# Attention 2: gathers issued back to back, and two norm chains placed one tile later on VectorE

## The reference

```
x = x + tanh(g_ffn[0]) * L0_ffn(layernorm(x))        # rows routed to 8 experts
x = x + tanh(g_xattn[1]) * L1_xattn(layernorm(x), ctx, ctx)
    # q = xn @ Wq + bq; softmax(q k^T / 4, masked) v @ Wo + bo; 16 heads of 16
x = x + tanh(g_ffn[1]) * L1_ffn(layernorm(x))
```

## Time and profile before

| | us |
|---|---|
| median of 3 runs | 718.93 (717.57 to 720.0) |
| profiled execution | 719.26 |
| its span in the trace | 717.8 |

### The profile page before, as it was taken

One profiled execution on the slowest core, in us unless ns is written; L12 is line 12 of the kernel. 1 busy time (PEld: TensorE's weight loads), 2 busy tenths in 40 slices (PEclk: granted clock), 3 DMA queues, 4 the chain that ended last, 5 costly groups with the idle time before them and its releaser, 6 DMA issues. The chain is left out here.

```text
span 717.8 us, 14149 instructions
## 1 busy us (share of the span) xinstructions
PE 640.2 (89%) x4630; PEld 578.3 (81%) x4631; DVE 455.3 (63%) x1183; ACT 288.6 (40%) x513; POOL 213.8 (30%) x335
## 2 busy tenths in 40 slices
PE   3989898999999999999767696699979899999996
PEld 3657677998998999898645466498978799999996
DVE  5855555878447635632498789856558774646575
ACT  7634252444334423233445425544315142434332
POOL 7361236200001000340265656540007301110163
PEclk9999899999999999999988999989989999999999
DMA  7999942765005720997310100000035200101124
GB/s 242 416 418 415 362 169 96 242 216 200 32 29 156 267 96 15 325 347 236 105 30 1 58 1 1 0 1 1 1 123 223 74 31 29 59 31 57 44 77 158
DMA packets 26464, 96.65 MB, mean 135 GB/s; under 512 B 6357, under 2 KB 11994, under 8 KB 20186
## 3 DMA queue, kind: packets, MB, share of 16 engines
q1 hardware_dynamic: 19402, 76.64, 29.1%
q0 software_dynamic: 6304, 18.88, 8.1%
q10 hardware_dynamic: 720, 0.66, 0.3%
HBM read 57.50 MB, written 44.96 MB: 143 GB/s over the span
## 5 line engine op out<-in xcount | busy, mean ns | idle before, releaser
L2328 ACT ACTIVATE vz<-psum,fb 128x256 f32<-128x256 f32 x112 | 52.7, 476 | 98.9 <-PE psum L53 98.6
L1795 ACT ACTIVATE e_h<-psum,e_be 128x256 f32<-128x256 f32 x84 | 39.2, 475 | 86.5 <-PE psum L53 66.0
L1895 DVE CAST e_h_hi<-e_h 128x256 fp32r<-128x256 f32 x84 | 24.6, 292 | 54.0 <-ACT e_h L1795 53.9
L2377 DVE TENSOR_TENSOR f_h_lo<-vz,f_h_hi 128x256 fp32r<-128x256 f32 x112 | 47.7, 426 | 3.8
L51 PE MATMUL psum<-e_h_hi,kz_hi 128*128 128x256 f32 x168 | 47.6, 283 | 0.0
L52 PE MATMUL psum<-e_h_lo,kz_hi 128*128 128x256 f32 x168 | 46.9, 279 | 0.0
L53 PE MATMUL psum<-e_h_hi,kz_lo 128*128 128x256 f32 x168 | 46.9, 279 | 0.0
L988 POOL TENSOR_TENSOR s_sc<-s_sc,s_top 128x1024 f32<-128x1024 f32 x16 | 30.5, 1905 | 39.6 <-DVE s_top L1113 39.6
L51 PE MATMUL psum<-kz_hi,s_qT_hi 128*128 128x256 f32 (+1 forms) x80 | 32.2, 402 | 11.2 <-DVE s_sc L1107 9.5
L2375 DVE CAST f_h_hi<-vz 128x256 fp32r<-128x256 f32 x112 | 33.9, 303 | 10.6 <-ACT vz L2328 10.6
L53 PE MATMUL psum<-f_gT_hi,f_w_lo 128*128 128x256 f32 x144 | 40.1, 279 | 0.0
(11 more groups left out here) (510 smaller groups left out, 2263.7 us busy)
## 6 DMA issues: line engine op xcount, KB each, us to landing
xs<-zeros SPq DMA_DIRECT2D x18, 1024.0 KB, 17.0
w_raw<-in_W SPq DMA_DIRECT2D x18, 1024.0 KB, 5.6
ys<-zeros SPq DMA_DIRECT2D x6, 1024.0 KB, 24.6
ys<-x_norm POOLq DMA_DIRECT2D x18, 256.0 KB, 2.6
w_raw<-in_W SPq DMA_DIRECT2D x8, 512.0 KB, 5.7
e_w1u<-in_W SPq DMA_DIRECT2D x4, 1024.0 KB, 7.3
f_w_lo<-fw SPq DMA_DIRECT2D x6, 512.0 KB, 6.7
x_norm<-xs POOLq DMA_DIRECT2D x10, 256.0 KB, 3.1
```

The costliest lines, as they stand in the source:

```text
L1795: nc.scalar.activation(h32[:, m % RING], ps[:, HIDDEN_BANKS[m % RING], 0:SLOT], ACT.Gelu, bias=be[:, m:m + 1]).then_inc(gelu_ok, 1)
L1895: nc.vector.tensor_copy(h_hi[:, m], h32[:, m % RING]).then_inc(hh_ok, 1)
L2328: nc.scalar.activation(h32[:, m % RING], ps[:, HIDDEN_BANKS[m % RING], 0:SLOT], ACT.Relu, bias=b1[:, f * MH + m:f * MH + m + 1]).then_inc( ...
L2377: nc.vector.tensor_tensor(h_lo[:, m], h32[:, m % RING], f32(h_hi[:, m]), ALU.subtract).then_inc(hl_ok, 1)
```

## The change

It has two parts. POOL no longer waits for the landing of the third batch's four gathers before it issues the fourth batch's four. On DVE the norm chain leaves the end of the r = 0 part of a tick and stands at the start of the r = 1 part of the next one. By its condition (`b < B - 2`) this holds for b = 0 and b = 1, so the chains of the third and of the fourth batch both move, from ticks 0 and 4 to ticks 1 and 5.

```
@@ -980,7 +980,6 @@
             head.gather(pool, 2)
-            pool.wait_ge(yg_ok[2], 16 * TB)
             head.gather(pool, 3)
@@ -1185,8 +1184,9 @@
                     if b:
                         head.add_rows(dve, b + 2)
                     sums(b + 2, 0)
-                    norm_chain(b + 2, 0)
                 if r == 1:
+                    if b < B - 2:
+                        norm_chain(b + 2, 0)
                     if b + 1 < B:
                         q_lo(b + 1)
```

## The result

Over 20 runs each, the changed kernel takes 720.87 us in the median (718.99 to 723.4) and the kernel before 717.23 (712.3 to 721.06). The ratio is 1.0047 (95% interval 1.0032 to 1.0062), 3.4 us at 717.2: slower, as forecast.

What follows compares the result with a forecast made beforehand. The prediction took DVE's queue to bound the loop in ticks 0 to 1 and 4 to 6. Gathers 0, chains +1.17 and +2.16 on 719.26 gave 722.6, or 722.2 for the median; range 720.0 to 724.0.

Steps and rivals of the forecast that it cites:

- The gathers cost and gain nothing in this order: Tick 0: tile 0's subtraction starts 0.9 us sooner, but DVE's own work hides it; worth 0.
- The third batch's chain, +1.17 us: Tick 1: the chain sits out POOL's work, taking 4.14 us instead of 2.97, so tile 2's mask comes 1.17 later.
- The 1.17 lasts: Ticks 1 to 3: the delay travels through POOL's multiplication of tile 1 and probs_T(1) to `xT_lo`, about 1.17 us late.
- The fourth batch's chain, +2.16: Tick 5: with the same POOL neighbours the chain takes 4.14 us instead of 1.98 in tick 4; +2.16 us.
- all that follows is 3.33 later: Behind `weighted(0, 0)`, which waits for `q_lo`: no fixed time absorbs the delay, so everything after comes 3.33 us later.
- The idle time of `weighted(0, 0)`: On PE, waiting for `q_lo`: a sign to check, about 6.5 us of idle time against 2.33 before.
- the stall on the two TENSOR_SCALARs: Chain's first two instructions, L872 and L874: these two of the ten sit out POOL's work, taking about 0.7 and 1.8 us.
- The absolute time: Whole kernel: 722.2 us forecast, from 722.6 for an execution like the profiled one, 0.33 above the median 718.93.
- the chain's second instruction does not slip in: Rival, ticks 1 and 5: L874 gets between POOL's two instructions, chain 2.49 us, total 719.0; 0.10 together with no stall.
- no gathers collide: Rival, at `add_rows`: the third batch's rows land late and it waits up to 2.1 us, up to 724.3; chance 0.07.
- the first delay is not lost: Rival, tick 3: two waits on DVE take up the 1.17, only 2.16 remain, 721.1; chance 0.16.

Runs made afterwards that it cites:

- chains_only: The change with the wait between the third and fourth batch's gathers put back, so only both norm chains move; 1.0044 of the kernel before.
- third_only: The change, but only the third batch's chain moves and the fourth's stays in tick 4; 718.1 us, 1.002 of the kernel before.
- change_again: The change itself timed once more, nothing altered; 720.42 us, 1.0041 of the kernel before.
- seed_early: The change, but both chains' L872 and L874 stay in ticks 0 and 4 and only the other eight instructions move; 1.0069 of the kernel before.
- half_pool: The change with POOL's subtraction and multiplication of ticks 1 and 5 each split in two by heads; 1.006 of the kernel before.
- gathers_only: The kernel before without the wait between the third and fourth batch's gathers, both norm chains left in place; 0.9985 of the kernel before.
- warm_again: The change with 28 unused transposes on PE ahead of weighted(0, 0), second timing; 719.32 us, 1.0037 of the kernel before.

## Why the prediction was right

- *The gathers cost and gain nothing in this order*: right. Tile 0's subtraction starts 0.90 us sooner after `add_rows` (3.74 against 4.64), as foretold, and nobody gains by it. `add_rows` starts without a wait, and `chains_only` has the change's masks. Alone the same edit takes away the stall in tick 0, which the prediction did not need to see.
- *The third batch's chain, +1.17 us*: +1.11 at mask 2. L872 and L874 read 0.68 and 1.82, as in the earlier trace rows.
- *The 1.17 lasts*: right, and by the path foretold. At tile 3's mask only 0.43 is left of it, but `xT_lo` is 1.11 later (24.02 against 22.91), and `third_only` carries 1.12 to mask 6. ACT's `norm_1` and tile 1's exponential were late as foretold (372.04 and 374.02) and held nobody up.
- *The fourth batch's chain, +2.16*: +2.1 (3.21 less 1.11).
- *What was mis-sized*: "all that follows is 3.33 later". Behind `weighted(0, 0)` there are 4.28, since the matmuls from mask 6 to mask 7 run longer at the lower clock, for 1.07 us. Nothing in the sum allowed for that. The 3.4 us at the end have an interval (2.3 to 4.4) that holds both 3.33 and 4.28, and behind mask 12 the 14 profiled executions of all the kernels take from 273.2 to 279.9 us each. So that 3.4 came out so near to 3.33 is partly luck, and what becomes of the other 0.9 us is open.
- *The idle time of `weighted(0, 0)`*: 6.5 us foretold, 5.57 in this trace and 6.57 in `change_again`. In this trace scores(6) ran at the lower clock and ended later; `weighted(0, 0)` itself starts at 41.94 and 41.95, so nothing hangs on the difference.
- *The reason was too narrow*: I laid the stall on the two TENSOR_SCALARs. L86 and L87 pay too when they come first, as `seed_early` shows, and L86 as the third with halves on POOL (`half_pool`); for L88 to L93 no run shows it. The number came out because in the change these two come first.
- *The absolute time*: 722.2 was built on a median of 718.93; 20 runs of the kernel before give 717.23. On these the same +3.3 is 720.5, and 720.87 was measured.
- *The rivals*: the chain's second instruction does not slip in (L874 reads 1.82 in both ticks), no gathers collide, and the first delay is not lost.

## What to carry to other kernels

Before a small chain is moved on VectorE, look at what GpSimd does at the new place: in this kernel ten instructions of 0.17 us took 4.1 us instead of 2.0 because two GpSimd instructions ran beside them. A twin of the moved work that already stood in such a place gave the price to a tenth of a us. And ask which engine the next wait really hangs on: the same stall cost its full length in ticks 1 and 5, while in tick 10 taking the whole chain away from between two masks gained only 0.28 us.

## What was not expected of the hardware

- GpSimd is held up too. With the gathers back to back, the last one starts while `add_rows` (358.75 to 360.03) runs on DVE and takes 1.90 us instead of 0.95; in `gathers_only`, where only the end of `add_rows` overlaps it, 1.26. A gather that started first was not delayed: 0.95 at 358.91 before, with `add_rows` from 359.19. The fourth batch's `add_rows` in the kernel before shows both sides, 1.73 instead of 1.28 on DVE and 2.89 instead of 1.90 on POOL:

```profile
387.04 1.73 DVE L854 SCALAR_TENSOR_TENSOR x_res<-x_norm,tg,x_res 128x1024 f32<-128x1024 f32 x1
```
```profile
387.65 2.89 POOL L992 TENSOR_TENSOR s_sc<-s_sc,s_rden 128x1024 f32<-128x1024 f32 x1
```

- Between two GpSimd instructions only one stalled DVE instruction got in at a time; two halves on GpSimd cost DVE no less than one whole (2.75 against 2.50 us).
- The idle time right ahead of a stretch on TensorE did not tell its clock. The same 33 matmuls took 6.59 us at 0.74 behind 2.33 us of idle time (before), 7.24 at 0.64 behind 1.06 (`third_only`), 7.66 at 0.61 behind 5.57 (the change), and 5.06 at 1.00 where transposes had filled most of the wait (`warm_again`).
